# A Mamba-style scan and cross-attention layer on one core: replicating transfers merged into one each with a repeated source, and q and k kept in DRAM in stacked row order

## The reference

```python
# 1. selective state space block, d_inner 512, 16 states, chunks of 64 tokens
xc, res = split(x @ W_in.T + b_in)
u = silu(causal_conv(xc, 3 taps) + conv_b)
dlt, B, C = split(u @ W_x.T, [64, 80])
delta = softplus(dlt @ W_dt.T + b_dt)
h[t] = exp(delta[t] * -exp(A_log)) * h[t-1] + delta[t] * B[t] * u[t]    # per feature d and state n
y[t] = sum over n of h[t] * C[t]
x = layernorm(x + (y * silu(res)) @ W_out.T + b_out)
# 2. cross-attention with 16 heads of 16 features over ctx
x = layernorm(x + softmax(q @ k.T / 4) @ v @ w_o.T + b_o)
# 3. eight experts, each for 32 tokens of every batch
x = layernorm(x + (silu(x @ w1) * (x @ w3)) @ w2)
```

## Time and profile before

| | us |
|---|---|
| time, median of 3 runs | 3154.16 (3147.67 to 3166.78) |
| the profiled execution's own time | 3166.08 |
| its span, first to last instruction | 3164.3 |
| GpSimd busy (mixers only) | 2104.7 |
| VectorE busy | 2251.5 |
| ScalarE busy | 1779.6 |
| TensorE busy (matmul) | 2586.5 |

### The profile page before, as it was taken

The page is one execution under the profiler, slowest core; times in us unless marked ns, Lnnn a source line. Parts: engine busy times, 40 slices in busy tenths (PEclk is TensorE's granted clock), DMA queues, the critical chain, the costliest instruction groups (busy, mean ns, idle before and its releaser), DMA issues. The chain is left out here.

```text
span 3164.3 us, 49706 instructions
## 1 busy us (share of the span) xinstructions
PE 2586.5 (82%) x14848; PEld 1773.8 (56%) x14848; DVE 2251.5 (71%) x3688; ACT 1779.6 (56%) x3817; POOL 2104.7 (67%) x1060
## 2 busy tenths in 40 slices
PE   3578788888888888888888888888887768999998
PEld 2345556556556656656556655656665545555564
DVE  2678888888888888888888888888888732222322
ACT  1556666766676666666666666667666431212212
POOL 0999888988888888898888888888888500000000
PEclk8788998998898989898998988999898769999999
DMA  3455555555555555555555555555555312111231
GB/s 91 125 139 139 142 145 144 147 142 144 141 156 145 154 143 158 149 157 148 144 154 144 145 141 143 152 151 153 149 142 139 92 46 82 54 54 54 65 98 27
DMA packets 253307, 398.86 MB, mean 126 GB/s; under 512 B 45329, under 2 KB 185617, under 8 KB 248946
## 3 DMA queue, kind: packets, MB, share of 16 engines
q1 hardware_dynamic: 249458, 393.57, 45.6%
q10 hardware_dynamic: 3584, 2.10, 0.3%
HBM read 300.08 MB, written 94.37 MB: 125 GB/s over the span
## 5 line engine op out<-in xcount | busy, mean ns | idle before, releaser
L416 POOL TENSOR_TENSOR dBu<-w_r,bc_r 128x1024 f32<-128x1024 f32 x512 | 1208.9, 2361 | 301.2 <-DMA w_r<-w_dram 297.6
L490 ACT ACTIVATE dA_ps<-delta_r,a_neg 128x252 f32<-128x252 f32 x2048 | 875.3, 464 | 428.1 <-DVE dA_ps L649 176.5
L626 DVE TENSOR_TENSOR_SCAN h<-dA_ps,dBu 128x512 f32<-128x512 f32 x704 | 845.9, 1216 | 224.1 <-ACT dA_ps L490 219.0
L426 POOL TENSOR_TENSOR h<-h,bc_r 128x512 f32<-128x512 f32 (+1 forms) x512 | 859.4, 1679 | 19.3 <-DVE h L626 19.2
L529 ACT ACTIVATE probs<-st_ps 128x512 f32<-128x512 f32 x512 | 299.2, 584 | 218.8 <-PE st_ps L769 218.4
L626 DVE TENSOR_TENSOR_SCAN dA_ps<-dA_ps,dBu 128x512 f32<-128x512 f32 x320 | 390.3, 1220 | 2.7 <-ACT dA_ps L490 2.2
L699 DVE TENSOR_REDUCE mx<-s_ps 128x2 f32<-128x512 f32 x512 | 344.4, 673 | 66.9 <-PE s_ps L769 66.3
L769 PE MATMUL a_ps<-xT,w_conv 128*128 128x256 f32 x1536 | 383.1, 402 | 0.0
L769 PE MATMUL y_ps<-h,sel 128*32 128x256 f32 x4096 | 278.5, 418 | 82.3 <-POOL h L426 82.3
L769 PE MATMUL s_ps<-k_st,q_st 96*128 96x256 f32 x1024 | 292.9, 370 | 47.2 <-DVE mx L699 46.9
L769 PEld LDWEIGHTS a_ps<-xT,w_conv 128*128 128x128 f32 x1536 | 297.1, 199 | 56.8 <-issue 16.1
(11 more groups left out here) (106 smaller groups left out, 3513.3 us busy)
## 6 DMA issues: line engine op xcount, KB each, us to landing
delta_r<-delta_dram SPq DMA_DIRECT2D x512, 128.0 KB, 3.0
w_r<-w_dram SPq DMA_DIRECT2D x512, 128.0 KB, 3.4
bc_r<-bc_dram SPq DMA_DIRECT2D x128, 256.0 KB, 5.6
q_st<-q_parts_dram SPq DMA_DIRECT2D x512, 64.0 KB
k_st<-k_parts_dram SPq DMA_DIRECT2D x512, 64.0 KB
delta_dram<-delta SPq DMA_DIRECT2D x32, 512.0 KB, 3.9
w_dram<-u SPq DMA_DIRECT2D x32, 512.0 KB, 5.8
k_parts_dram<-parts SPq DMA_DIRECT2D x32, 512.0 KB, 3.4
```

Source lines behind the costliest of these rows:

```text
L416: pool.tensor_tensor(dBu[:, n % NB], w_r[:, n // RP % 2, t % RP].unsqueeze(1).to_broadcast([P, QS, L]), bc_r[:, b.par, 0], ALU.mult).then_ ...
L426: pool.tensor_tensor(h[:, n % NH, states], h[:, n % NH, states], bc_r[:, b.par, 1, states], ALU.mult).then_inc(s_hC, 1)
L490: last = nc.scalar.activation(dA[n % NDA][:, q, :, 1:], delta_r[:, n // (2 * RP) % 2, t % RP].rearrange("p (c t) -> p c t", t=CH)[:, :, 1: ...
L626: nc.vector.tensor_tensor_scan(dst, decays, dBu[:, n % NB, 2 * half:2 * half + 2].rearrange("p q t -> p (q t)"), 0.0, ALU.mult, ALU.add).t ...
```

## The change

- `replicate` and `bc_load` issue one transfer for each tile in place of four. The destination is all 128 partitions, the source repeats the 32 rows four times (for B and C each of four rows 32 times) by a step of zero. The semaphore counts go from 128 to 32 per part and from 64 to 16 for B and C.
- The tensors for q and k in DRAM get the order of the stacks: [feature block, 64 stack rows, 8 heads, 256]. For this the rows of w_q and w_k and their biases are turned, so that the partitions of `parts` are (feature in head, head), and `parts` has the feature block ahead of high and low.
- q is stored by two transfers and k by four, since every part stands in two of the four row groups. The stack load of four heads is one transfer of 64 rows of 4 KB for q, one for k, and the row of ones: 3 instead of 9.

The core of the diff:

```diff
@@ bc_load
                 rows = bc_dram[b.par].rearrange("(j a q) t -> j (a q t)", j=4, a=2)
-                for j in range(4):
-                    dst = bc_r[CT * j:CT * (j + 1), b.par].rearrange("p a q t -> p (a q t)")
-                    sp.dma_start(dst, rows[j].partition_broadcast(CT)).then_inc(s_bc[b.par], 16)
+                src = rows.unsqueeze(1).to_broadcast([4, CT, 2 * QS * L])
+                dst = bc_r[:, b.par].rearrange("p a q t -> p (a q t)")
+                sp.dma_start(dst, src).then_inc(s_bc[b.par], 16)
@@ replicate
                     for tile, dram in ((delta_r, d_dram), (w_r, w_dram)):
                         src = dram[b.par].rearrange("(i s) c -> i (s c)", s=4)[:, cols]
-                        for j in range(4):
-                            dst = tile[CT * j:CT * (j + 1), n % 2].rearrange("p g t -> p (g t)")
-                            sp.dma_start(dst, src).then_inc(s_rep[part], 16)
+                        src = src.unsqueeze(0).to_broadcast([4, CT, RP * L])
+                        dst = tile[:, n % 2].rearrange("p g t -> p (g t)")
+                        sp.dma_start(dst, src).then_inc(s_rep[part], 16)
@@ store_parts, now store_q and store_k
-                    dst = dram[b.par].rearrange("c (m p) t -> p c m t", p=P)
-                    sp.dma_start(dst, parts[:].bitcast(F32)).then_inc(done, 16)
+                for twice in range(2):
+                    dst = q_dram[b.par].rearrange("m (c w i) h t -> w (i h) m c t", c=2, w=2)[twice]
+                    sp.dma_start(dst, parts[:].bitcast(F32)).then_inc(s_q_dram, 16)
...
+                for twice in range(2):
+                    for m in range(KD):
+                        dst = k_dram[b.par, m].rearrange("(w c i) h t -> w (i h) c t", c=2, w=2)[twice]
+                        sp.dma_start(dst, parts[:, m].bitcast(F32)).then_inc(s_k_dram, 16)
@@ load_stack
-                    for row in range(4):
-                        rows = slice(DK * row, DK * row + DK)
-                        for stack, dram, part in ((q_st, q_dram, row // 2), (k_st, k_dram, row % 2)):
-                            src = dram[b.par, part].rearrange("(h i) t -> i h t", i=DK)[:, heads, :]
-                            sp.dma_start(stack[rows, heads, :].bitcast(F32), src).then_inc(s_stack[gr], 16)
+                    for stack, dram in ((q_st, q_dram), (k_st, k_dram)):
+                        src = dram[b.par, gr // 2, :, HG * (gr % 2):HG * (gr % 2) + HG]
+                        sp.dma_start(stack[0:4 * DK, heads, :].bitcast(F32), src).then_inc(s_stack[gr], 16)
@@ layouts
+    turned = np.arange(D).reshape(KD, P // DK, DK).swapaxes(1, 2).reshape(-1)
-        "w_q": columns(i["xattn_w_q"].T, D), "w_k": columns(i["xattn_w_k"].T, D),
+        "w_q": columns(i["xattn_w_q"][turned].T, D), "w_k": columns(i["xattn_w_k"][turned].T, D),
```

More of the change, by code:

```diff
@@ L190, in mixers @@
         ctxT = sb("ctxT", [P, KD, L])
-        parts = sb("parts", [P, 2, KD, L], F32R)
+        parts = sb("parts", [P, KD, 2, L], F32R)
         v = sb("v", [P, 2, TT, H, 2 * DK])
@@ L263, in mixers @@
         N_SET = 9 + NDA + 3 + TAPS * KD
-        STACK_DMAS = 9
+        STACK_DMAS = 3
         X2_DMAS = P // EC
@@ L340, in load_ctx, with store_q, store_k @@
                 sp.dma_start(ctxT[:], src).then_inc(s_ctxT, 16)
[L342 to L346, removed]
-                    dst = dram[b.par].rearrange("c (m p) t -> p c m t", p=P)
-                    sp.dma_start(dst, parts[:].bitcast(F32)).then_inc(done, 16)
-                return piece
+            def store_q(b):
+                wait_all(sp, (s_q_hi, 1, b, 1), (s_q_lo, 1, b, 1),
+                         *[(s, STACK_DMAS * 16, b.back(2), STACK_DMAS * 16) for s in s_stack])
+                for twice in range(2):
+                    dst = q_dram[b.par].rearrange("m (c w i) h t -> w (i h) m c t", c=2, w=2)[twice]
+                    sp.dma_start(dst, parts[:].bitcast(F32)).then_inc(s_q_dram, 16)
+            def store_k(b):
+                wait_all(sp, (s_k_hi, 1, b, 1), (s_k_lo, 1, b, 1),
+                         *[(s, STACK_DMAS * 16, b.back(2), STACK_DMAS * 16) for s in s_stack])
+                for twice in range(2):
+                    for m in range(KD):
+                        dst = k_dram[b.par, m].rearrange("(w c i) h t -> w (i h) c t", c=2, w=2)[twice]
+                        sp.dma_start(dst, parts[:, m].bitcast(F32)).then_inc(s_k_dram, 16)
             def load_stack(gr):
@@ L382, in _ @@
                 (O_OUT - 2, load_x_tok),
[L383 removed]
+                (O_K + 1, store_k),
                 (O_N1 + 1, store_x1),
                 (O_XP + 1, bc_store),
[L386 removed]
+                (O_Q + 1, store_q),
                 *[(O_LD + HG * gr, load_stack(gr)) for gr in range(NG)],
@@ L391, in _ @@
             sp.wait_ge(s_x2_st, 16 * B * X2_DMAS)
-            sp.wait_ge(s_q_dram, 16 * B)
-            sp.wait_ge(s_k_dram, 16 * B)
+            sp.wait_ge(s_q_dram, 32 * B)
+            sp.wait_ge(s_k_dram, 64 * B)
             sp.wait_ge(s_m_dram, 16 * B * NG)
@@ L411, in piece @@
                     n = b.value(NU, t)
-                    pool.wait_ge(s_rep[t // 4], b.value(128, 128))
-                    pool.wait_ge(s_bc[b.par], b.same_parity(64))
+                    pool.wait_ge(s_rep[t // 4], b.value(32, 32))
+                    pool.wait_ge(s_bc[b.par], b.same_parity(16))
                     if n >= NB:
@@ L513, in norm, with high @@
                 return piece
-            def high(s_mm, s_hi, s_dram, steps_back):
+            def high(s_mm, s_hi, s_dram, per, steps_back):
                 def piece(b):
@@ L518, in piece @@
                     if b.back(steps_back):
-                        act.wait_ge(s_dram, b.back(steps_back).value(16, 16))
-                    nc.scalar.activation(parts[:, 0], a_ps[:], ACT.Copy).then_inc(s_hi, 1)
+                        act.wait_ge(s_dram, b.back(steps_back).value(per, per))
+                    nc.scalar.activation(parts[:, :, 0], a_ps[:], ACT.Copy).then_inc(s_hi, 1)
                 return piece
@@ L679, in piece @@
                     dve.wait_ge(s_hi, b.value(1, 1))
-                    nc.vector.tensor_tensor(parts[:, 1], a_ps[:], parts[:, 0].bitcast(F32),
+                    nc.vector.tensor_tensor(parts[:, :, 1], a_ps[:], parts[:, :, 0].bitcast(F32),
                                             ALU.subtract).then_inc(s_lo, 1)
@@ L1198, in decoder_layer @@
     x2_dram = nc.dram_tensor("x2_rows", (E * ET, D), F32, kind="Internal").ap()
-    q_dram = nc.dram_tensor("q_parts_dram", (2, 2, D, L), F32, kind="Internal").ap()
-    k_dram = nc.dram_tensor("k_parts_dram", (2, 2, D, L), F32, kind="Internal").ap()
+    q_dram = nc.dram_tensor("q_stack_dram", (2, KD, 4 * DK, P // DK, L), F32, kind="Internal").ap()
+    k_dram = nc.dram_tensor("k_stack_dram", (2, KD, 4 * DK, P // DK, L), F32, kind="Internal").ap()
     m_dram = nc.dram_tensor("max_rows_dram", (NG, 2, HG * L), F32, kind="Internal").ap()
@@ L1242, in layouts @@
     bias_rows(32, 2, b_in[DI:].reshape(ND, 1, P))
-    bias_rows(64, 2, np.concatenate([i["xattn_b_q"], i["xattn_b_k"]]).reshape(4, 1, P))
+    bias_rows(64, 2, np.concatenate([i["xattn_b_q"][turned], i["xattn_b_k"][turned]]).reshape(4, 1, P))
     rows[96:98, 0:D], rows[96:98, D:2 * D], rows[96:98, 2 * D:2 * D + P] = i["attn_b_out"], i["xattn_b_o"], 1.0
```

16 lines of the change are left out of this document (7 added, 9 removed).

## The result

| | before | after |
|---|---|---|
| median of the runs, us | 3158.5 (3147.7 to 3166.8, 4 runs) | 4101.2 (4084.2 to 4133.9, 4 runs) |
| ratio after / before | | 1.302 (95% interval 1.298 to 1.306) |
| span of the profiled execution, us | 3164.3 | 4132.1 |

The account below looks back on a forecast made before the run. GpSimd, delayed by late replication, was taken to bound the mixers. Delays of 3.6 (part 1), 5.0 (part 3) and 10.1 us (part 0) made 18.7 per batch, times 31.5 = 590 us, giving 3750 us, range 3400 to 4250.

Parts of the forecast that it names:

- GpSimd sets the pace and loses to late replication: Mixers: GpSimd's 65.6 us busy plus 9.3 us waiting for `w_r` make 75 of a batch's 76 us.
- Four engines: Replicating transfers: the source's 4 outermost rows confine each to four of 16 DMA engines, 105 GB/s together.
- The time of a pair: One part's delta and w, 1.05 MB: 10.0 us on four engines plus 1.7 for landing, 11.7 instead of 8.1.
- Part 2 hidden: Part 2 waits for part 1 on the four engines, done near 1541, used at 1541.17 + 3.6, costing nothing.
- The waits: GpSimd's waits for parts in each batch: part 1 3.6 us later, part 3 5.0, part 0 10.1 new.
- q's way to DRAM behind B and C: q's stores queue behind B and C's 10.0 us, delaying the stack load; part 0 lands at 1599.5 instead of 1580.85.
- The second copy of q and k: q and k written twice: 1.05 MB more per batch on sixteen engines; q's two stores taken as 3.0 us.
- Four engines as the bound: Rival, chance 0.10: contention near 17 GB/s per engine, 103 us or more per batch, 4050 to 4500 us.
- Sixteen engines as a rival: Rival, chance 0.13: the destination's 128 rows decide, a pair takes 6.7 us, 4.6 us saved per batch, time 3007.
- What was named as a sign: Expected after the change: `w_r` wait near 890 us, late `bc_r`, DMA share 0.25 at 105 GB/s, longer SyncE wait for q.
- Share 0.25 but only 70 GB/s: Sign in stretches while a part is loaded: the rate assumed per engine, 26.2 GB/s, was wrong.

Follow-up runs that it names:

- 32 outermost: The changed kernel with partitions reordered so delta and w sources are [32, 4, 1024], and B and C repeat 32 outermost; 3082.3 us, ratio 0.976.
- 4 distinct: The changed kernel with delta and w read as four differing row sets outermost instead of one repeated, values wrong; 4111.0 us, ratio 1.303.
- the good setting: The changed kernel with delta, w, B and C replicated by four transfers each, against the kernel before; 3128.2 us, ratio 0.991.
- the bad: The kernel before with only delta, w, B and C replicated by one transfer each, 4220.3 us, against the changed kernel, 4101.2 us.
- the runs with part 1 sooner: Part 1's replication moved two slots forward in SyncE's order: with 32 outermost 3063.3 us, ratio 0.970; in the kernel before 3098.1 us, ratio 0.983.

## Why the prediction came out as it did

The forecast was slower by 19%, 3750 us with 3400 to 4250; measured are 4101 us and 30%. Direction, mechanism and place were right, the size too small by over a third. The time also lies just outside the forecast's own 3500 to 4050 and inside the 4050 to 4500 of a rival with a chance of 0.10, so it is the wide range that held it. Step by step:

- **GpSimd sets the pace and loses to late replication: right for the change, too simple for a gain.** 927 of the 968 us that came in are GpSimd's wait on `w_r`. In the other direction the claim fell short: taking part 1's lateness away gave 56 us (3154.5 to 3098.1) and not 150 to 190, as VectorE was close behind. The prediction had read this off the waits as if nothing would follow.
- **Four engines: right**, shown by the share of 0.25 to 0.27, by 5 steps on the semaphore instead of 16, by 32 outermost (3082 us) and by 4 distinct (4111 us). The inference from ScalarE's closing packets and the single engine at the start held for a source and a destination that differ.
- **The time of a pair: the term that was mis-sized.** Parts 3, 0 and 1 land after 14.1, 16.9 and 16.0 us (medians) where 11.7, 12.5 and 11.7 were forecast. The rate of 26.2 GB/s for each engine, taken from the earlier trace rows, holds for the later microseconds of a transfer (102 to 105 GB/s for four); early in it four engines move 64 to 81, down to 16 each, a little under the 16.9 that the prediction gave as the bottom. And where the sum had 1.7 us for start and landing together, the first data alone comes some 2 us after the issue.
- **Part 2 hidden: right**, GpSimd's median wait there is 0.0.
- **The waits**: forecast 5.0 at part 3, 13.3 at part 0 (3.2 and 10.1 more), 9.6 at part 1 (6.0 and 3.6 more), in all 27.9; measured 7.5, 19.2 and 12.8 (medians), in all 39.5. The largest gap is at part 0, where the later issue and the longer landing add up.
- **q's way to DRAM behind B and C: right in kind, short in size.** From part 3's issue to part 0's 33.1 us go by instead of 28.9 forecast, since part 3 and B and C each take longer than the 10 us of the sum. With B and C off the four engines 5.9 of them went.
- **The second copy of q and k**: its cost was right (q lands some 3 us later with it), the sign of the whole half was not. The prediction counted the saved issues of the stack load (2.9 us), which give the 3 us back, but nothing for the parts themselves, which land 0.6 to 1.4 us sooner than with q and k as before. The half gained 26 us in the good setting and 119 in the bad.
- **Four engines as the bound, the rival whose range holds the time**: its period was 103 us or more, and 105.1 is measured, but for another reason. Between 500 and 3300 us of the trace no DMA packet is in flight 17% of the time, and four or more are 74% of it. So the four engines are busy at most some 78%, within the 71 to 80% that the forecast had for them (67 to 76 of 94.7 us): loaded, and not the bound. The time is lost in waits one behind another.
- **Sixteen engines as a rival**: it would have given 3007 by the prediction's price. The run with 32 outermost is that case and measured 3082; 4.6 us per batch were forecast and 2.2 measured. Part 1 stays late there (5.5 us), behind the norm and the store of x2, and the runs with part 1 sooner show how little is left to gain before VectorE is the limit.
- **What was named as a sign**: GpSimd's wait near 890 us in some 90 waits (1224.5 in 95), `bc_r` landing after over 11 us (23), parts on a share of 0.25 (right) at 105 GB/s (70 to 102 in the windows shown), busy time unchanged (right), SyncE waiting much longer for q (191.9 against 85.6 us, right). "Share 0.25 but only 70 GB/s", the sign of a wrong rate, came in one of the three windows.

## What to carry to other kernels

Before merging several transfers into one, look at the outermost dimension of both sides: a small count there takes engines away from the whole transfer, whether it counts a repetition or distinct rows. A large count outermost (here [32, 4] in place of [4, 32], at the price of another order of partitions, which only tables on the host had to follow) does not, not even when it is the repetition. The DMA share of a stretch in which one transfer is in flight tells how many engines carry it. And where the profile names one wait for the whole gap, ask which engine comes next before counting the wait as a gain.

## What the runs showed of the hardware

- An issue on SyncE can last 10 to 14 us (median 11.05 us, against 0.44) when much is queued on few DMA engines, and the issue that stands is the next one in order, whatever it is. With q stored once it was 1.9 us, and SyncE waited for q instead.
- Four DMA engines that are busy all the time moved 64 to 105 GB/s, 16 to 26 GB/s each, with the others idle, less in the first microseconds of a transfer than later; the reason stays open.
- A transfer with 4, 8 or 32 outermost on one side and 32 or 128 on the other completed in 5, 9 or 16 steps on its semaphore.
- With TensorE idle for longer, its granted clock fell: 0.76 over the mixers against 0.90, and its busy time rose by 307 us with the same instructions. Over the mixers, in 3.5 us without a matmul, and in the stretch behind those, where 0.50 is the lower level of 1.2 GHz:

```profile
66.00:3300.00 3234.00, 2158.00 (x12051) 1477.50 (x12049) 1946.99 (x3049) 1542.39 (x3373) 1991.29 (x1000) 0.76 0.36 114
2066.00:2069.50 3.50, 0.00 (x0) 0.00 (x0) 1.64 (x3) 0.42 (x2) 0.00 (x0) 0.59 0.17 62
2069.50:2074.00 4.50, 0.71 (x1) 0.28 (x1) 0.00 (x0) 0.00 (x0) 0.00 (x0) 0.50 0.78 195
```

TensorE has slack in this kernel, and no run here shows that the slower clock cost time.
